# One more drain on GpSimd in the last round of a graph-attention kernel

## The reference

```python
q, k, v = h @ Wq, h @ Wk, h @ Wv                      # h is x
e = sum_d(k[src] * q[dst]) / sqrt(64)                 # one score per edge and head
attn = softmax of e over the edges with the same dst  # segment_max, exp, segment_sum
a = segment_sum(attn * v[src], dst)
o = a @ Wo                                            # zero for a node without edges
y = layernorm(h + o, ln1_g, ln1_b)
f = relu(y @ W1 + b1) @ W2 + b2
r = layernorm(y + f, ln2_g, ln2_b)
return layernorm(x + r)                               # without gain and offset
```

## Time and profile before

| what | value |
|---|---|
| median of 3 runs | 683.18 us (682.54 to 683.65) |
| span of the profiled execution | 682.0 us |
| median less that span | 1.2 us |
| busy: PE, DVE, ACT, POOL | 94%, 85%, 77%, 59% |
| DMAs issued by GpSimd in the last 82 us of the span | 30 |

### The profile page before, as it was taken

How to read it: one execution, slowest core, us unless ns; L and a number is a source line. 1 busy time by engine, 2 the same in 40 slices (tenths; PEclk the granted TensorE clock), 3 DMA queues, 4 the chain that set the end, 5 groups by cost and what they waited for, 6 DMA issues and landing times. The chain is left out here.

```text
span 682.0 us, 10864 instructions
## 1 busy us (share of the span) xinstructions
PE 641.5 (94%) x3520; PEld 483.8 (71%) x3520; DVE 578.0 (85%) x1391; ACT 528.3 (77%) x1140; POOL 401.7 (59%) x363
## 2 busy tenths in 40 slices
PE   5999999999999999999999999999999999999950
PEld 2778877777777777777777777777778778675520
DVE  7668769879898898898889889988989898899792
ACT  2525269877888987988798889878878999698881
POOL 7267244867675865756776574864547726735423
PEclk9999999999999999999999999999999999999995
DMA  7844154644643745674474456455554824536452
GB/s 227 220 101 133 44 123 106 173 122 142 148 121 131 159 121 148 167 157 92 146 177 117 113 161 137 105 168 123 127 128 155 184 62 135 139 77 138 131 113 91
DMA packets 37747, 91.44 MB, mean 134 GB/s; under 512 B 8346, under 2 KB 9642, under 8 KB 37690
## 3 DMA queue, kind: packets, MB, share of 16 engines
q0 software_dynamic: 31536, 82.74, 47.6%
q1 hardware_dynamic: 6154, 8.01, 4.3%
HBM read 71.20 MB, written 20.99 MB: 135 GB/s over the span
## 5 line engine op out<-in xcount | busy, mean ns | idle before, releaser
L558 ACT ACTIVATE squares<-rows,nmean 125x512 bf16<-125x512 f32 x200 | 142.3, 713 | 41.5 <-DVE nmean L902 19.8
L412 POOL DMA_INDIRECT x_rows<-in_x_dram,node_idx x40 | 48.2, 1205 | 56.8 <-DVE rows L917 47.3
L416 POOL DMA_INDIRECT out_dram<-rows,node_idx x40 | 46.4, 1160 | 56.4 <-ACT rows L618 47.0
L473 POOL DMA_DIRECT2D x_rows<-in_L_gnn_ln_b_dram x40 | 52.9, 1372 | 31.1 <-DVE rows L821 21.7
L898 DVE SCALAR_TENSOR_TENSOR rows<-pF,rows 125x512 f32<-125x512 f32 x78 | 50.6, 686 | 23.2 <-PE pF L1103 22.5
L963 PE MATMUL pP<-wo_hi,aT_hi 128*125 128x512 f32 x160 | 65.9, 412 | 0.3 <-DVE aT_lo L848 0.3
L963 PE MATMUL pP<-xTs_hi,wv_hi 128*128 128x500 f32 x160 | 65.8, 411 | 0.0
L963 PE MATMUL pP<-xTd_hi,wq_hi 128*128 128x500 f32 x160 | 65.4, 409 | 0.1
L963 PE MATMUL pP<-xTs_hi,wk_hi 128*128 128x500 f32 x160 | 63.5, 397 | 0.6 <-ACT q L539 0.6
L963 PE MATMUL pP<-wo_lo,aT_hi 128*125 128x512 f32 x160 | 63.1, 394 | 0.0
L963 PE MATMUL pP<-wo_hi,aT_lo 128*125 128x512 f32 x160 | 63.0, 394 | 0.0
(11 more groups left out here) (197 smaller groups left out, 1760.6 us busy)
## 6 DMA issues: line engine op xcount, KB each, us to landing
x_rows<-in_L_gnn_ln_b_dram POOLq DMA_DIRECT2D x40, 512.0 KB, 6.7
dst_row<-in_dst_dram SPq DMA_DIRECT2D x9, 250.5 KB
q<-in_L_gnn_Wq_dram SPq DMA_DIRECT2D x1, 1024.0 KB, 5.6
rows<-in_L_gnn_Wk_dram SPq DMA_DIRECT2D x1, 1024.0 KB, 7.8
rows<-in_L_gnn_Wv_dram SPq DMA_DIRECT2D x1, 1024.0 KB, 6.8
x_rows<-in_L_gnn_Wo_dram SPq DMA_DIRECT2D x8, 128.0 KB, 6.0
xd<-in_x_dram,dst_idx POOLq DMA_INDIRECT x40, 4.6
xs<-in_x_dram,src_idx POOLq DMA_INDIRECT x40, 3.8
```

What stands on the lines that cost most here:

```text
L412: pool.indirect_dma_start(rows, None, x, bass.IndirectOffsetOnAxis(ap=table[:, column:column + 1].bitcast(U32), axis=0), bounds_check=N - ...
L416: pool.indirect_dma_start(out, bass.IndirectOffsetOnAxis(ap=table[:, column:column + 1].bitcast(U32), axis=0), rows, None, bounds_check=N ...
L473: pool.dma_start(xr_wide[n], bass.AP(tensor=be2.tensor, offset=be2.offset, ap=[[0, P], [0, 2], [1, D]]), accum_op=ALU.add).then_inc(s[f"be ...
L558: ins = act.activation(squares[:, t, :], w[n][:, t, :], ACT.Square, bias=nmean[c][n][:, t:t + 1], accum_out=sq[c][n][:, t:t + 1])
```

## The change

PLAN gets one step, SETTLE, on GpSimd, and the loop over GpSimd's steps executes `pool.drain()` for it. The drain waits for no semaphore and signals none.

```diff
-E1.be 137892 148033 145283 185994 265480; E1.out 149056 150533 151501 241974 302224
+E1.be 137892 148033 145283 185994 265480; E1.out 149056 150533 151501 241974 302224; !SETTLE 358570
...
+                elif step == "SETTLE":
+                    pool.drain()
```

## The result

| | before | changed |
|---|---|---|
| median | 682.78 us (5 runs, 682.54 to 683.65) | 677.21 us (5 runs, 677.08 to 677.48) |
| span of the profiled execution | 682.0 us | 675.5 us |

The medians differ by 5.6 us, which is 0.82%. The ratio is 0.9913, with a 95% interval of 0.9901 to 0.9925; it is taken against the 683.18 us of the first three runs of the kernel before. So the changed kernel is faster by 0.8 to 0.9%. Forecast were 677.4 us and faster.

What follows compares the result with a forecast made beforehand. The prediction took GpSimd's closing drain, 6.52 us fully exposed, as what ends the kernel: 682.0 - 6.52 + 0.7 = 676.2 us span, plus 1.2 us gives 677.4 us. Range 676.7 to 678.7; 8 in 10, 676.5 to 679.8.

Steps and rivals of the forecast that it cites:

- The end is the closing drain, not the last scatter: At the block's end, GpSimd's drain runs 6.52 us exposed after the last scatter has landed; nothing else runs.
- The price belongs to DMAs on record: GpSimd's drain settles one by one the DMAs issued and not yet settled; 6.33 us of the closing drain.
- 0.7 us is left: Closing drain after the change: eight records at 0.065 us plus 0.19 us for an empty drain.
- bounds on one record: Price of one DMA record in GpSimd's drain: between 0.020 and 0.21 us.
- The added drain ends at 657.7 to 657.8 and costs N1 0.0 to 0.1 us: New drain after the last adds: settling overlaps waiting for the newest add, ending when N1's scatter rows are ready.
- rival A: The new drain first waits for the adds, then settles for 6.52 us, ending at 664.2; 679.4 us, chance 0.13.
- The cover of 3.78 us behind N1, and 4.5 in all: Last scatters on GpSimd: N1 may be 3.78 us late before E0, with 0.74 more before E1, without moving the end.
- Slower beside busy engines: New drain beside busy VectorE: factors of 1.10 and 1.72 give 7.2 and 11.2 us, both inside the cover.
- The 1.2 us of the median above the span: Whole kernel: 1.2 us added to the predicted span of 676.2 us to get the measured median.
- my saving of 5.8 us: Whole kernel: the closing drain falls from 6.52 to 0.7 us, saving 0.85%.
- Rival B: Closing drain stays 6.5 us, its price belonging to no record or to the block's closing; 683.2 us, chance 0.11.
- C: A fixed 6.5 us starts after the adds land and the old drain stays full; 685.2 us, chance 0.06.

Runs made afterwards that it cites:

- experiments 1 and 2: First: changed kernel with the added drain moved earlier, 30, 59, 94 or (two drains) 145 DMAs behind it: 679.51, 680.90, 683.60, 684.01 us. Second: see experiment 2.
- k = 8: The changed kernel itself, with 8 DMAs issued by GpSimd between the added drain and the closing one: 677.21 us.
- k = 59: Changed kernel with the added drain moved ahead of the last round's first add, 59 DMAs issued behind it: 680.90 us in one run.
- Experiment 4: Changed kernel with waits for the landing of the three adds put ahead of the added drain: median 678.97 us.
- experiment 2: Kernel before with one more drain behind the waits for the last landings, right ahead of the block's end: 682.78 us in one run.

## Why the prediction was right, step by step

- *The end is the closing drain, not the last scatter.* Right: this row shrank by 5.81 us, the medians differ by 5.6, and nothing else took its place at the end.
- *The price belongs to DMAs on record.* Right, shown by experiments 1 and 2.
- *0.7 us is left.* Measured 0.709. The number came out by luck of two errors: 0.065 us a record was too small (0.082), 0.19 us for an empty drain too large (0.04), and at k = 8 they cancel. At k = 59 the same terms miss by 0.9 us. Both my bounds on one record held it, but neither named the truth: nothing in the trace of before says that the record stops growing at about 80 DMAs.
- *The added drain ends at 657.7 to 657.8 and costs N1 0.0 to 0.1 us.* This step failed. It ended at 659.95 and N1 was 3.1 us late. The landing itself came as I had it, 8.7 us behind the issue for 8.5. But I had settling and waiting overlap in full, and rival A had them not overlap at all; in fact the last 2.95 us came behind the landing. With the landing at 657.0, full overlap would have made it 7.1 us long (from 649.92), A 13.6 us (657.0 + 6.52); it took 10.0.
- *The cover of 3.78 us behind N1, and 4.5 in all.* Right, and it is what made the time right in spite of the failed step. How much was to spare differs between executions: 3.1 us of lateness and 0.6 us of longer issues used 3.7 of 3.78 us in one trace, some 0.9 us were left in another. Experiment 4 overran it and paid what lay beyond it.
- *Slower beside busy engines.* I allowed a factor of up to 1.72; experiment 4 shows none.
- *The 1.2 us of the median above the span.* Every run on record lies about 1.7 us above its own span (677.21 and 675.5 for the changed kernel's profile), so the profile of the kernel before, with its 682.0, was of an execution of about 683.7 us. That did no harm, since span and term together are the first median, 683.18. From the median of five, 682.78, my saving of 5.8 us gives 677.0; 677.21 was measured.
- Rival B is out by experiment 2; C with it. Rival A's time, 679.4, is what the kernel costs when the waits are written in (678.97).

## What to carry to other kernels

When the chain of waits ends well before the span does, look at the rows of the block's end: on GpSimd the closing drain cost 0.04 us here and 0.082 us for each DMA issued since its last drain, up to 6.5 to 7.1 us, and all of it behind the last landing. A drain of one's own in an idle stretch of GpSimd takes that away, if only few DMAs follow it and nothing behind it is in a hurry. Reckon its end as its full price after the last issue or half its price after the landing of the newest DMA in flight, whichever is later, and check that against the idle time of what is queued behind it. More such drains brought nothing measurable here.

## What the runs showed of the hardware that I had not expected

- The price of a drain on GpSimd stops growing: 7.13 us at 94 DMAs, 6.51 at 145, 6.52 at 322, and 5.87 at 314 with three adds as the newest. What sets the limit stays open.
- At least half of a drain's price comes after the landing of the newest DMA, however long that one was in flight: 2.95 us in the changed kernel, 0.36 us for eight DMAs. One drain, with 118 on record, had only 2.42 us there; that stays open.
- The row of a drain opens while the instruction ahead of it still runs (648.3 against 649.92), so its length is not its price: 11.67 us on the row, 10.0 us of GpSimd's time.
